# Sixty-one spare identity products and an earlier pair of Gram products in a two-half fp32 kernel

## What is computed

```
x = embed[tokens] + PE                       # the tower: D = 128, 8 heads of 16, 2 layers
for i in range(2):
    h = LN(x); q, k, v = h @ Wq, h @ Wk, h @ Wv
    k, v = causal_conv(filters, k), causal_conv(filters, v)
    g = relu(<v k^T, gate>)^2 + EPS          # one gate for a token and head
    o = q . cumsum(g v k^T) / (cumsum(g) + EPS);  o = o / |o|
    x = x + o @ Wo
    x = x + gelu(LN(x) @ W1) @ W2
h = LN(x) @ out_k + out_b                    # 256 columns
n = LN(h)                                    # the second half: 16 heads of 64, no softmax
h = h + concat(q (k^T v) / 8) @ Wo           # q, k, v from n
n = LN(h); h = h + (silu(n @ Wg) * (n @ Wu)) @ Wd
```

## Time and profile before

| | us |
|---|---|
| median of 3 runs | 1856.96 (1856.71 to 1857.99) |
| the profiled execution | 1858.16 |
| its span, first to last instruction | 1856.3 |
| TensorE busy in the span | 1793.9 (97%) |
| VectorE busy | 1095.9 (59%) |
| ScalarE busy | 727.6 (39%) |
| GpSimd busy | 425.4 (23%) |
| mean granted TensorE clock | 0.988 of full |

### The profile page before, as it was taken

One profiled execution on the slowest core, in us unless ns is written; L12 is line 12 of the kernel. 1 busy time (PEld: TensorE's weight loads), 2 busy tenths in 40 slices (PEclk: granted clock), 3 DMA queues, 4 the chain that ended last, 5 costly groups with the idle time before them and its releaser, 6 DMA issues.

```text
span 1856.3 us, 40349 instructions
## 1 busy us (share of the span) xinstructions
PE 1793.9 (97%) x16378; PEld 1544.7 (83%) x16378; DVE 1095.9 (59%) x2955; ACT 727.6 (39%) x1508; POOL 425.4 (23%) x391
## 2 busy tenths in 40 slices
PE   6899999999999999879999999999999999999998
PEld 5788888888888888768888888888888888888877
DVE  4678888888888888566435434443444444344443
ACT  2445555555555555434333223223223323332232
POOL 4323333333333221110120211211221121012112
PEclk8899999999999999989999999999999999999999
DMA  3000000000100001011000000000000000000000
GB/s 101 10 7 20 17 19 19 19 19 19 30 19 19 15 13 70 29 38 66 1 24 24 24 1 24 24 18 7 24 24 1 24 24 24 1 24 23 10 15 23
DMA packets 29349, 42.29 MB, mean 23 GB/s; under 512 B 6000, under 2 KB 22768, under 8 KB 29168
## 3 DMA queue, kind: packets, MB, share of 16 engines
q1 hardware_dynamic: 26160, 35.07, 5.8%
q0 software_dynamic: 2048, 4.20, 0.9%
q10 hardware_dynamic: 960, 0.46, 0.1%
HBM read 22.93 MB, written 16.78 MB: 21 GB/s over the span
## 4 chain that ended last, share of the span: by engine, by line
PE 85%; DVE 10%; issue 2%; POOL 1%; DMA 1%; ACT 1%; SPq 0%; DVEq 0%; POOLq 0%; ACTq 0%
PE ps L1702 15%; PE ps L1703 14%; PE ps L1704 14%; PE ps L1288 5%; PE ps L1080 4%; PE ps L1752 4%; PE ps L1232 3%; PE ps L1769 3%; PE ps L1081 3%; PE ps L1082 3%; DVE att L939 3%; PE ps L1216 3%; PE ps L1268 2%; PE ps L1165 2%; PE ps L1716 2%
## 5 line engine op out<-in xcount | busy, mean ns | idle before, releaser
L1539 POOL TENSOR_TENSOR hids_low<-hid,hids_high 128x512 fp32r<-128x512 f32 x96 | 123.9, 1291 | 717.1 <-ACT hids_high L1688 716.8
L781 POOL TENSOR_TENSOR rstd<-var,minus_half 128x4 f32<-128x4 f32 x80 | 82.1, 1026 | 449.2 <-DVE var L868 449.0
L1019 ACT ACTIVATE xn<-x,shift,rstd 128x128 f32<-128x128 f32 x320 | 131.6, 488 | 120.4 <-DVE shift L873 120.4
L939 DVE TENSOR_TENSOR att<-ps,causal 128x512 f32<-128x512 f32 x256 | 158.6, 682 | 9.3 <-PE ps L1216 9.2
L1288 PE MATMUL ps<-w_f,wide 128*128 128x128 f32 x1024 | 128.0, 279 | 0.0
L1288 PEld LDWEIGHTS ps<-w_f,wide 128*128 128x128 f32 x1024 | 120.2, 193 | 5.4 <-issue 5.0
L1688 ACT ACTIVATE hids_high<-hid 128x512 fp32r<-128x512 f32 x96 | 60.3, 629 | 163.5 <-PE ps L1704 117.1
L1589 DVE COPY t<-ps 128x512 f32<-128x512 f32 x64 | 44.1, 691 | 125.5 <-PE ps L1752 77.7
L1682 ACT ACTIVATE silu<-ps 128x512 f32<-128x512 f32 x96 | 57.2, 596 | 145.1 <-PE ps L1704 114.9
L1702 PE MATMUL ps<-wd_high,hids_high 128*128 128x256 f32 x384 | 112.0, 292 | 0.7 <-POOL hids_low L1539 0.7
L1617 DVE TENSOR_TENSOR hid<-silu,ps 128x512 f32<-128x512 f32 x96 | 64.7, 684 | 80.4 <-PE ps L1704 57.8
(11 more groups left out here) (358 smaller groups left out, 4930.9 us busy)
## 6 DMA issues: line engine op xcount, KB each, us to landing
h_rows<-h_out SPq DMA_DIRECT2D x16, 512.0 KB, 2.7
h<-h_rows SPq DMA_DIRECT2D x16, 512.0 KB, 3.9
out<-bxn SPq DMA_DIRECT2D x32, 256.0 KB, 2.6
emb<-in_embed,idx POOLq DMA_INDIRECT x64
taps<-in_filters SPq DMA_DIRECT2D x1, 1024.0 KB
stage<-in_W_vT SPq DMA_DIRECT2D x2, 512.0 KB, 5.3
wk<-in_W_kT SPq DMA_DIRECT2D x1, 1024.0 KB, 4.9
wo<-in_W_oT SPq DMA_DIRECT2D x1, 1024.0 KB, 8.4
```

The lines of the kernel that those rows point to most:

```text
L781: pool.tensor_tensor(rstd[s][:], var[s][:], minus_half[:], ALU.pow)\
L939: dve.tensor_tensor(masked[:, :, PAIR * g:PAIR * g + PAIR, :], bank("qk", s, l, j, g, t)[:].rearrange("p (n r t) -> p n r t", n=2, r=PAIR) ...
L1019: act.activation(xn[s][:, j, :], x[s][:, j, :], ACT.Identity, bias=shift[s][:, j:j + 1], scale=rstd[s][:, j:j + 1]).then_inc(xn_made[s].se ...
L1539: pool.tensor_tensor(hids[1][:, halves, :], hid[:, half, :], hids[0][:, halves, :].bitcast(F32), ALU.subtract).then_inc(hid_low[s].sem, 1)
```

## The change

All numbers of the tables are ten times as large and some steps have others. Sorted, the order differs from the one before only between the last steps of the tower and the first of the second half. A new table `KEEP_BUSY` lists 14 steps of the tower with a number of spare products each, 61 in all. Ahead of such a step TensorE waits for the identity and positions to have landed, waits for the PSUM bank that the step will write, multiplies the 128x128 identity by itself into that bank so many times in plain fp32, and only then comes to the step and to the step's own waits. The step overwrites the bank. The entries are (step, group, layer, part, products).

```diff
+KEEP_BUSY = [("turn", 0, 0, 0, 14), ("kv", 0, 0, 0, 4), ("turn_v", 0, 0, 0, 3), ("wo", 0, 0, 0, 2),
+             ("turn_v", 1, 0, 0, 2), ("turn", 0, 1, 0, 4), ("unit", 1, 0, 0, 5), ("turn", 15, 1, 0, 4),
+             ("wo", 14, 1, 0, 2), ("turn", 14, 3, 0, 3), ("f1", 14, 1, 0, 4), ("av", 15, 1, 0, 9),
+             ("unit", 15, 1, 0, 3), ("wo", 15, 1, 0, 2)]
...
+        busy = {(step, g % (STREAMS if step in of_tower else B_STREAMS), l, j,
+                 g // (STREAMS if step in of_tower else B_STREAMS)): n for step, g, l, j, n in KEEP_BUSY}
+
+        def keep_busy(pe, step, *turn):
+
+            ring, name, _, _ = (tower.claims if step in of_tower else claims)(step, *turn)[0]
+            if step in of_tower:
+                pe.wait_ge(tower.pos_in, tower.pos_loaded)
+            uses.wait_free(pe, name)
+            for _ in range(busy[(step, *turn)]):
+                pe.matmul(bank(*name)[:, 0:P], ident[:], ident[:], start=True, stop=True)
+
...
             for step in order:
+                if step in busy:
+                    keep_busy(pe, *step)
```

A line or two of the tables, as they change (the old number ten times would be the same place):

```diff
-           (0, "b_turn", 0, 0, 11615), (0, "b_high", 0, 0, 13301), (0, "b_low", 0, 0, 12520),
...
+           (0, "b_xn", 0, 0, -839), (0, "b_turn", 0, 0, 116100), (0, "b_high", 0, 0, 125143),
```

More of the change, by code:

```diff
@@ L33 @@
 GK_SLOTS, ATT_SLOTS = 1, 2
[L36 to L48, removed]
[3 rows of a table removed]
[L52 to L64, removed]
[3 rows of a table removed]
[L68 to L71, removed]
@@ L361 @@
-PREPARE = [("w_load", 0, 120890), ("w_high", 0, 174686), ("w_low", 0, 185536), ("w_load", 1, 171478),
-           ("w_high", 1, 175669), ("w_low", 1, 191798), ("w_load", 2, 189317), ("w_high", 2, 194710),
-           ("w_low", 2, 195458), ("w_load", 3, 194680), ("w_high", 3, 195058), ("w_low", 3, 195626),
-           ("w_load", 4, 198355), ("w_scale", 4, 195646), ("w_high", 4, 198432), ("w_low", 4, 198121),
-           ("w_load", 5, 199146), ("w_scale", 5, 196732), ("w_high", 5, 198915), ("w_low", 5, 198122),
-           ("w_load", 6, 199232), ("w_scale", 6, 198122), ("w_high", 6, 199412), ("w_low", 6, 201689),
-           ("w_load", 7, 203352), ("w_scale", 7, 198204), ("w_high", 7, 199413), ("w_low", 7, 201702),
-           ("w_load", 8, 203355), ("w_scale", 8, 199588), ("w_high", 8, 200708), ("w_low", 8, 201790),
-           ("w_load", 9, 213284), ("w_scale", 9, 201792), ("w_high", 9, 200742), ("w_low", 9, 205622),
-           ("wk_load", 0, 165961), ("wo_load", 0, 172020)]
@@ new lines @@
+PREPARE = [("w_load", 0, 1208900), ("w_high", 0, 1746860), ("w_low", 0, 1856040), ("w_load", 1, 1714780),
+           ("w_high", 1, 1756690), ("w_low", 1, 1861178), ("w_load", 2, 1878632), ("w_high", 2, 1948982),
+           ("w_low", 2, 1956848), ("w_load", 3, 1878669), ("w_high", 3, 1950813), ("w_low", 3, 1957028),
+           ("w_load", 4, 1983550), ("w_scale", 4, 1962654), ("w_high", 4, 1980110), ("w_low", 4, 1980726),
+           ("w_load", 5, 1985210), ("w_scale", 5, 1980723), ("w_high", 5, 1981160), ("w_low", 5, 1981552),
+           ("w_load", 6, 1987323), ("w_scale", 6, 1981881), ("w_high", 6, 1981294), ("w_low", 6, 1997623),
+           ("w_load", 7, 2003656), ("w_scale", 7, 1983921), ("w_high", 7, 1981324), ("w_low", 7, 2016579),
+           ("w_load", 8, 2033550), ("w_scale", 8, 2016579), ("w_high", 8, 1999323), ("w_low", 8, 2017953),
+           ("w_load", 9, 2132840), ("w_scale", 9, 2017920), ("w_high", 9, 2007420), ("w_low", 9, 2056220),
+           ("wk_load", 0, 1659610), ("wo_load", 0, 1720200)]
@@ new lines @@
+START_UP = [("first", 0, -1011100), ("first", 1, 163500), ("first", 2, 163500), ("first", 3, 411600),
+            ("kv_rows", 0, -493020), ("kv_bias", 0, -405400), ("kv_scale", 0, -493020), ("kv_high", 0, 200930),
+            ("kv_add", 0, -493000), ("kv_low", 0, -493000), ("q_bias", 0, -214490), ("q_scale", 0, -493000),
+            ("q_high", 0, 200940), ("q_add", 0, -493000), ("q_parts", 0, -493000), ("q_low", 0, -493000),
+            ("gate_spread", 0, -144400), ("f1_bias", 0, 228960), ("f1_scale", 0, 162550), ("f1_high", 0, 226310),
+            ("f1_add", 0, -96500), ("f1_low", 0, 253450), ("head_rows", 0, -327310), ("head_bias", 0, 262060),
+            ("head_scale", 0, 253450), ("head_high", 0, 311600), ("head_add", 0, 253450), ("head_low", 0, 349110)]
@@ L469 @@
     minus_half: object
+    pos_in: object
+    pos_loaded: int
     ps: list
```

575 lines of the change are left out of this document (320 added, 255 removed), and 80 rows, old and new, of tables (MOVED_A, MOVED_B, PLACES_A, PLACES_B).

## The result

| | us |
|---|---|
| changed kernel, median of 15 runs | 1850.67 (1844.72 to 1855.6) |
| kernel before on the same chip, median of 15 runs | 1856.9 (1853.99 to 1858.6) |
| ratio, 95% interval | 0.9967 (0.9959 to 0.9976) |
| profiled execution: time, span, mean granted clock | 1850.68, 1848.8, 0.991 |

The change makes the kernel 6.2 us faster, 0.33%. Forecast were 1844.7 us and a range of 1839 to 1852 us: the sign and the range hold, but half of the forecast gain is missing. The runs spread over 11 us, those of before over 5.

The account below looks back on a forecast made before the run. TensorE, 85% of the chain of waits, was taken as the bound, slowed by half clock after short waits. Terms 2.0 + 2.8 + 1.8 + 2.7 + 3.0 = 12.3 off 1858.16 gave 1845.9, as median 1844.7 us; range 1839 to 1852.

Parts of the forecast that it names:

- half clock behind any filled gap: Sign of being wrong in the changed kernel's profile: then the number of products or the cause is wrong.
- 57.27 to 64.99: `qk`, `gate` and four `f1`, 7.72 us mostly at half clock, take 4.9 at full clock: 2.8 us gained.
- 773.94 to 781.08: Nine `f1` products, a `turn` and 16 `f2` records, 7.14 us, take 4.45 at full clock: 2.7 us gained.
- 78.20 to 84: 15 products behind `unit`, with five spares in the wait of 1.53, at full clock: 1.8 us gained.
- The first place to 35: 14 spares before the first `turn` cost 0; clock held, group 0's `mask` at 29.3 instead of 31.33: 2.0 us gained.
- The fall at 36 to 42: Half-clock stretch with no spare between the first `turn_v` and it: counted 0, with 2 us kept for the range.
- The seam: From group 15's `gated` to the first `t1`: 28.7 us instead of 31.8, `t1` 3.0 us earlier.
- Its four groups of products go at full clock, 2.8: `f1` of group 15, no Gram products among its groups: 2.8 us, ending at 821.75 instead of 824.72.
- Behind the seam: Exchanges in the second half, `attn` before `gram` and `w_low` among `m_low`, stand where TensorE has work queued: 0.
- the slower rival: Nine half-clock spares hold `av`; ScalarE waits at `w_high` for a load landing after 823: 1862.8 us, chance 0.05.
- The rival by which the clock falls in two of the places all the same: Spares are few and idle remains around each; two terms of 2.7 go: 1850.1 us, chance 0.2.
- The rival by which short gaps are not the cause, or identity products do not hold the clock: Terms 2.0 to 2.7 gone, 1 lost at the first `turn`, seam gives 3.0 - 2: 1857 us, chance 0.08.

Follow-up runs that it names:

- the middle's spares: Thirteen spare products ahead of turn of group 15 and wo, turn, f1 of group 14; changed kernel without them: 1854.55 us, ratio 0.9994.
- Spares alone: Kernel before, in its old order, with only `KEEP_BUSY` and the code of `keep_busy` added: 1844.39 us, ratio 0.9947.
- the first profile: First profiled execution of the unaltered changed kernel: 1850.68 us, span 1848.8; median of its runs 1850.67.
- the repeat: Changed kernel run again unaltered, on another group's chip: 1844.10 us, ratio 0.9945 to before.
- the third group: Four kernels on one chip, before 1855.43 us: thirteen spares removed 1854.55, no seam spares 1846.36, seam filled 1844.50, changed kernel unaltered 1852.58.
- the order alone: Changed kernel's new order with `KEEP_BUSY` empty, so no spare products: 1852.03 us, ratio 0.9989 to before.
- the third profile: Changed kernel run unaltered a third time, over 12 runs: 1852.58 us, ratio 0.9988 to before.
- the kernel without any seam spares: Changed kernel without the first 14, the av nine and five ahead of unit and wo of group 15, w_gateT loads before store: 1846.36 us.
- the loads first: Two w_gateT loads ahead of group 15's store, third w_low ahead of f2_out; in four kernels; as the changed kernel's only alteration 1843.46 us, ratio 0.9938.
- the three together: Changed kernel without the 14 ahead of the first turn and nine ahead of av, w_gateT loads ahead of the store: 1840.60 us, ratio 0.9929.

## Why the prediction was right, and where it was off

**The mechanism** (a short wait of TensorE, then dense work at half clock; spare products keep the clock up) is shown for two of the places. Behind the `qk` of 57.27 the clock is at half in the two profiles without spares and at full in all twelve with them. At `f1` of group 14 it is at half in the three without the middle's spares and at full in the eleven with them, and taking out those thirteen products alone brought the fall back. Spares alone gave 9.9 us. At `unit` of group 1 the effect is weaker: nine of the twelve profiles with spares still have 3.4 us of half clock there, where before had 6.8. The prediction names "half clock behind any filled gap" as a sign of being wrong; why these five spares do less is open.

**57.27 to 64.99, said 2.8**: 4.98 instead of 7.72, 2.7. Right. **773.94 to 781.08, said 2.7**: 4.34 instead of 7.14, 2.8. Right. **78.20 to 84, said 1.8**: 1.3 in the first profile, where the clock is at half from 74.8 to 78.2, and 2.1 in the repeat (from `unit` at 73.29 to `conv` at 77.15), where that stretch ended at 73.9, ahead of the products behind `unit`. Right in size.

**The first place to 35, said 2.0 with no cost of the 14**: right where the clock went as assumed (`mask` 29.09 in the repeat; forecast 29.3), wrong in the first profile (33.82). The step that failed is the one that lets the clock rise once within the row of spares and then takes it that "nothing is late". The 14 bring nothing: without them `mask` is at 29.2. And a completion of `kv` that comes late, which the sum has nowhere, undid the gain: in three of the eight profiles with fill there (products in seven, transposes in one) it is 1.8 to 3.9 us late, with `conv` at 24.45, 25.90 and 23.08; in the five others `conv` starts at 21.2 to 21.4. In the six profiles without fill, that of before among these, it is 0.4 and 0.9 late in two, both of the third group, and `conv` starts between 21.98 and 22.99. What delays the completions is not settled. Lateness goes with the chip or the time of the measurement, since every profile of the third group has it and none of the first and second; that the 14 make it worse is argued from the sizes here and from the spreads of the third group, not shown.

**The fall at 36 to 42, said 0, 2 in the range**: it stayed in all profiles but one. The fall at 169 was not forecast to move; with no spare near it, it is gone in seven profiles and there in seven, spares alone among these, and is worth 0.85.

**The seam, said 3.0**: 3.0 earlier became 1.3 later, and from the end of `gated` to `t1` it is 33.1 us instead of the forecast 28.7. The idle 4.41 was filled as reckoned; three other steps failed.
- The order by itself. Without the nine the prediction has the seam some 5.0 shorter; the order alone makes it 2.9 shorter (35.1 against 38.1), although `f1` ran at full clock there (2.9 us) as assumed. The clock fell at 806.1 instead, so `wo` took 0.9 longer and most of the Gram products ran at half. And ScalarE has both `gram_high` ahead of the `xn` of LayerNorm 3, which the prediction does not price: from `wo_out` to the transpositions it is 5.8 us there and 4.9 in after, 4.4 before. That the 2.9 is close to the 3.0 is luck.
- The nine spares were put at 2.6 with the fall at about 797 as before. In the first profile the clock fell earlier in the seam, behind the idle 1.80 ahead of the moved transpositions, and all nine went at half: 4.1. Where they ran at full clock (the repeat) they take 2.2 and the seam is 36.0; with none of them, and the rest as in after, it is 35.2. "Some 2 more" without the nine was right in sign; it is 0.8 to 4. Whether the clock falls behind that idle 1.80 does not hang on the nine: of the eleven profiles that have it the clock stood through `av` in three, the repeat, the third profile, and the kernel without any seam spares.
- `f1` of group 15. "Its four groups of products go at full clock, 2.8" fails in all eleven profiles with the new order and spares: they take 4.3 to 5.3, 4.4 in the first profile. There `wo` and the first Gram products were at half as well.

**Behind the seam, said 0**: the prediction followed the third `w_load` past the `store` of group 14, and ended at `t1`. The `w_gateT` loads moved behind group 15's `store` and the third `w_low` behind the last `low`. With that order the stretch behind `t1` is 0.95 us longer on average, with the loads first 0.4. The step that failed is the 0 for what is exchanged behind `t1` because TensorE "has work queued". The `w_high` wait of the slower rival did stay hidden (ScalarE starts it at 817.40).

**Second half**: 1.7 us less from `t1` to the end than before, though nothing was changed there that should save. Over the profiles this stretch varies from 1024.8 to 1029.9 us; the three of the changed kernel have 1026.4, 1025.0 and 1028.4, before 1028.1. One source is TensorE's waits for `xns_low` (total, number, longest), from 928 to 1728 us in before and from 922 to 1722 in after:

```profile
PE ps L1702 <- DVE xns_low L1576: 2.2, 3, 1.0
```

```profile
PE ps L1736 <- DVE xns_low L1610: 1.2, 2, 1.0
```

The total is 2.2 us in before and 1.2 in after; the unaltered kernel's third profile has 2.0 again. So the 1.7 us are within what varies from profile to profile, and no gain of the change can be read from them.

**The sum.** Said were 12.3 us, the profile gives 7.5 (1856.3 to 1848.8). Missing are 4.3 in the seam, 2.4 at the start (0.4 later by 57.7 instead of 2.0 earlier) and 0.5 at 78; unforecast came 0.85 at 169 us and 1.7 in the second half. The median of before's 15 runs lies 1.3 under its profiled one, hence 6.2. Over three measurements the changed kernel is 6.2, 9.5 and 2.9 us under before; the forecast 12.3 lies above all of them, and only the three together, 13.0, reach it. The profiles of the three differ mostly in the first 31 us, in the seam and in the second half. The rival by which the clock falls in two of the places all the same, 1850.1, named the time, but not the mechanism: the half-clock stretches that made it lie mostly in the first 31 us and in the seam, not at the two filled places with a term of 2.7. The rival by which short gaps are not the cause, or identity products do not hold the clock, fell: spares alone gave 9.9 us, and the fall at 773 came back without the middle's spares.

## What to carry to other kernels

Fill short waits ahead of dense TensorE work with a few spare products, and only such as end before the wait does. Put none where the step behind can already start: nine there made the seam 0.8 us longer at full clock and 4 at half. When an order is changed, follow every queue to the end of the loads that moved, behind the point where the change seems to stop; and profile more than once, since the clock's falls and single waits differ from run to run.
